# Slot rows of 272 floats instead of 257 in the two mixture stages of an eight-layer kernel

## The reference

```python
topk_idx, topk_w = _gate(xf, gate_w, gate_bias)        # 2 of 8 experts for each token
g = jax.nn.silu(jnp.einsum('th,ehi->tei', xf, w_gate)) # I = 128
u = jnp.einsum('th,ehi->tei', xf, w_up)
experts_y = jnp.einsum('tei,eih->teh', g * u, w_down)
masked_y = jnp.take_along_axis(experts_y, topk_idx[:, :, None], axis=1)
y = jnp.einsum('tkh,tk->th', masked_y, topk_w)
shared = jax.nn.silu(x @ sw_gate) * (x @ sw_up) @ sw_down
return y + shared
```

## Time and profile before

| | us |
|---|---|
| median of three runs | 3938.58 |
| the profiled execution | 3947.42 |
| its span, from the first to the last instruction | 3945.4 |
| PE busy | 3244.7 |
| DVE busy | 2616.1 |
| POOL busy | 1533.2 |
| mean granted TensorE clock | 0.917 of full speed |

### The profile page before, as it was taken

How to read it: one execution, slowest core, us unless ns; L and a number is a source line. 1 busy time by engine, 2 the same in 40 slices (tenths; PEclk the granted TensorE clock), 3 DMA queues, 4 the chain that set the end, 5 groups by cost and what they waited for, 6 DMA issues and landing times. The chain is left out here.

```text
span 3945.4 us, 55387 instructions
## 1 busy us (share of the span) xinstructions
PE 3244.7 (82%) x15992; PEld 1825.7 (46%) x15993; DVE 2616.1 (66%) x5017; ACT 1717.3 (44%) x3399; POOL 1533.2 (39%) x1586
## 2 busy tenths in 40 slices
PE   7898889888699698898979898776596787997495
PEld 3343334333256534434344466453374475664274
DVE  6999899999877585757668575974146673224145
ACT  5757666566355355554636553112032232222031
POOL 4898888988600212212121101534353100002533
PEclk8999999999999889798989999888798898998797
DMA  4555455565400000000000002601144792000236
GB/s 132 139 139 136 126 138 138 131 137 133 108 1 0 15 2 2 1 2 1 2 1 2 1 1 85 164 0 41 56 146 132 178 124 33 16 11 9 88 99 200
DMA packets 370273, 283.07 MB, mean 72 GB/s; under 512 B 214027, under 2 KB 290367, under 8 KB 370017
## 3 DMA queue, kind: packets, MB, share of 16 engines
q1 hardware_dynamic: 356960, 246.43, 25.5%
q0 software_dynamic: 13056, 33.65, 2.5%
HBM read 205.69 MB, written 76.16 MB: 71 GB/s over the span
## 5 line engine op out<-in xcount | busy, mean ns | idle before, releaser
L608 POOL TENSOR_TENSOR mamba_dBu<-mamba_du,mamba_bcs 128x512 f32<-128x512 f32 x512 | 640.3, 1272 | 127.6 <-DMA mamba_bcs<-mamba_bc 85.7
L531 PE MATMUL mamba_banks<-mamba_hc,ident 128*128 128x512 f32 x1024 | 537.8, 634 | 144.6 <-DVE mamba_hc L847 144.5
L777 ACT ACTIVATE mamba_banks<-mamba_delta,mamba_a_neg 128x512 f32<-128x512 f32 x512 | 352.3, 690 | 181.9 <-DVE mamba_hc L847 171.0
L1542 DVE TENSOR_REDUCE attn_mp<-attn_banks 128x1 f32<-128x512 f32 (+3 forms) x768 | 384.0, 551 | 69.0 <-PE attn_banks L1252 48.8
L531 PEld LDWEIGHTS mamba_banks<-mamba_hc,ident 128*128 128x128 f32 x1024 | 180.8, 195 | 459.1 <-DVE mamba_hc L847 346.6
L847 DVE TENSOR_TENSOR mamba_hc<-mamba_banks,mamba_bcs 128x512 f32<-128x512 f32 x512 | 344.3, 674 | 11.4 <-PE mamba_banks L531 11.4
L840 DVE TENSOR_TENSOR_SCAN mamba_banks<-mamba_banks,mamba_dBu 128x512 f32<-128x512 f32 x256 | 312.1, 1219 | 56.1 <-ACT mamba_banks L777 36.5
L840 DVE TENSOR_TENSOR_SCAN mamba_banks<-mamba_banks,mamba_h_end,mamba_dBu 128x512 f32<-128x512 f32 x256 | 327.3, 1279 | 20.1 <-ACT mamba_banks L777 12.2
L1249 PE MATMUL attn_banks<-attn_kT,attn_qT 96*128 96x512 bf16 (+3 forms) x768 | 272.3, 374 | 12.3 <-ACT attn_kT L1431 4.9
L1264 PE MATMUL attn_banks<-attn_qT,attn_kT 98*128 98x512 bf16 (+3 forms) x768 | 247.3, 341 | 12.5 <-ACT attn_r L1450 4.8
L939 PE MATMUL ffn_hp<-ffn_xT,ffn_w1T 128*128 128x512 f32 x512 | 231.3, 607 | 10.9 <-ACT ffn_xT L160 7.5
(11 more groups left out here) (389 smaller groups left out, 6665.9 us busy)
## 6 DMA issues: line engine op xcount, KB each, us to landing
mamba_bcs<-mamba_bc SPq DMA_DIRECT2D x256, 512.0 KB, 5.0
moe_slots_moe<-moe_pad SPq DMA_DIRECT2D x2, 9252.0 KB, 55.6
moe_xg<-moe_slots_moe SPq DMA_DIRECT2D x144, 128.5 KB
mix_qkv<-mixA_qkv SPq DMA_DIRECT2D x8, 1536.0 KB, 5.9
mixA_y<-moe_rows SPq DMA_DIRECT2D x16, 512.0 KB, 5.8
mix_qk<-mix_qkv SPq DMA_DIRECT2D x16, 512.0 KB, 7.7
mix_v<-mix_qkv SPq DMA_DIRECT2D x16, 256.0 KB, 7.6
mix_out<-mixB_oh SPq DMA_DIRECT2D x16, 256.0 KB, 6.9
```

The costliest lines, as they stand in the source:

```text
L531: pe.matmul(banks[:, SUMS + k % PAIR, :], c.ident[:, :], hc[:, n % RING, :], start=False, stop=True, skip_group_check=True).then_inc(sem(" ...
L608: pool.tensor_tensor(dBu[:, n % RING, :], du[:, v, k, :], bcs[:, i_of(n) % 4, 0, :], ALU.mult)\
L777: act.activation(banks[:, n % RING, :], delta[:, v, k, :], ACT.Exp, scale=a_neg[:, k, st:st + 1])\
L1542: dve.tensor_reduce(mp[:, qt // GT, j, qt % GT, at // 512:at // 512 + 1], banks[:, item % SLOTS, 0:size], AX.X, ALU.max).then_inc(sem("rin ...
```

## The change

`ROW` goes from `D + 1` = 257 floats (1028 bytes) to `D + 16` = 272 floats (1088 bytes, 17 times 64). The index stays at column `D`. What grows with it: the rows in DRAM of both `moe_slots` tensors, `moe_rows` (`xr`), `moe_xg`, and `moe_pad`. The 15 floats behind the index are zeroed once in each stage by a new memset on POOL, with a wait for it.

```diff
-ROW = D + 1
+LINE = 16
+ROW = D + LINE
@@
+        tail_ready = s.sem("tail_ready")
@@
                         pool.tensor_tensor(shift[:, at], minus[:, at], rstd[:, at], ALU.mult).then_inc(shift_ready, 1)
+                    pool.memset(xr[:, :, D + 1:ROW], 0.0).then_inc(tail_ready, 1)
+                    pool.wait_ge(tail_ready, 1)
                     pool.wait_ge(m["xd_padded"], 32)
@@
-                                pool.tensor_copy(xr[:, t:t + CHUNK, D:ROW].bitcast(U32).rearrange("p t o -> p (t o)"),
+                                pool.tensor_copy(xr[:, t:t + CHUNK, D:D + 1].bitcast(U32).rearrange("p t o -> p (t o)"),
@@
-                        pool.indirect_dma_start(yd, bass.IndirectOffsetOnAxis(ap=xg[:, i % XRING, D:ROW].bitcast(U32), axis=0),
+                        pool.indirect_dma_start(yd, bass.IndirectOffsetOnAxis(ap=xg[:, i % XRING, D:D + 1].bitcast(U32), axis=0),
@@
-    out["moe_pad"] = np.concatenate([np.zeros((P, D), np.float32), np.ones((P, 1), np.float32)], axis=1)
+    out["moe_pad"] = np.concatenate([np.zeros((P, D), np.float32), np.ones((P, LINE), np.float32)], axis=1)
```

## The result

The changed kernel took 3949.75 us (median of 20 runs), the kernel before took 3941.49 us on the same chip (median of 20). The ratio is 1.0017, with a 95% interval of 1.0009 to 1.0024: a small loss, 7 to 8 us, real but inside the 0.3% that the prediction counted as no change. The profiled execution of the changed kernel took 3957.95 us with a span of 3956.0 us.

A forecast was written before the change was run, and what follows sets the result against it. POOL's scatter issue, PE's shared expert, then the routed experts' ring were taken to bound the mixture stages. Slot loads -0.5, shifted tiles +1, the rest 0: +0.5 us, so 3939 us against the median, range 3923 to 3954.

The forecast's parts named there:

- Memset, scatters: Mixture stages on POOL: memset 0.41 us hidden in a 36 us wait, scatter issue unchanged at 0.960 us; both 0.
- The fill: Two DMAs in `lin` filling slot rows: 5.8% more bytes, landing long before POOL's only wait for it; 0 either way.
- The 77 and 58 us: The fill in `lin`: cost of 5.8% more bytes at 63.6 or 48.0 us a MB.
- The slot loads: Routed experts' ring: 22 waits, 15.5 us in all; each load 0.036 us less or 0.027 more; -0.5 us taken.
- the lower price: Slot loads: 48.0 us a MB, read from plain 1024-byte rows, against 55.2 for 1028-byte rows.
- the 15% for a packet: `mix_heads`: upper end for a dearer packet on shifted tiles, 1.26 us a set, 15 us over 12 sets.
- The tiles that move: `mix_heads` tiles shifted by 32 bytes: dearer packets would show as DVE store waits; 0 to +12 us, +1 taken.
- the 3 us that SP's queue was said to be able to fall behind: `mix_heads`: slack before DVE waits for a store, taken off the 15 us over 12 sets.
- The price of a packet: `mix_heads`: 12.4 ns a packet before; over 14 ns would show the prediction wrong.
- the case: Rival: `mix_heads` becomes bound by its DMAs, from about 15% a packet; 3961 us at 25%; chance 0.12 for over 0.3%.
- The rule of the Trainium skill: Pieces fetched from the 256-byte boundary below: slot loads +1.5 us in place of -0.5; `mix_heads` pieces some 20% more beats.
- The standstill: Rival: unaligned rows stop PE during the mixture stages' scatters; even rows save 83 us, 3856 us; chance 0.06.

The follow-up runs named there:

- rows-only kernel: The changed kernel with 224 bytes of unused SBUF ahead of the `mix` tiles, which so stand as before modulo 256 bytes; ratio 0.9995 to the kernel before.
- shift-only kernel: The kernel before, 257-float rows kept, with 32 bytes of unused SBUF ahead of the tiles of `mix`; ratio 1.0022.
- with four buffers: Four buffers of `mixB_oh` in place of two, a semaphore each; on one chip 3862.3 us on the changed kernel, 3861.3 us on the kernel before.
- `mixB_oh` alone: The kernel before with only `mixB_oh` shifted by 32 bytes, the other tiles in place modulo 256; ratio 1.0013.
- one-tile kernels: The kernel before with `mix_qk`, `mix_v` or `mixB_oh` alone shifted by 32 bytes; the three ratios add up to 1.0044.

## Why the prediction was right, and where a term was off

*Memset, scatters.* Right: 0.50 us (0.41 forecast) in a wait of 36 us; 0.960 us a scatter, as before.

*The fill.* Cost nothing, as said, and was dearer in neither of the two ways. Queue q1 over 80 us from the issue of the fill, changed kernel (2459:2539) and rows of 264 floats (2455:2535):

```profile
q1 hardware_dynamic: 19771, 20.59, 83.8%
```

```profile
q1 hardware_dynamic: 19723, 19.96, 80.0%
```

0.838 x 80 x 16 / 20.59 = 52.1 us a MB, and 51.3 for the 1056-byte rows, against 63.6 us; the 63.6 is the highest of the eight traces with 1028-byte rows, the others give 58.8 to 60.7 over the same 80 us. So a multiple of 32 bytes is enough. Longer rows landed sooner, and nobody waits for them. The 77 and 58 us in the prediction are sums that don't come out: 60 bytes on each of 18432 rows are 1.1 MB, 70 and 53 us at its two prices. Nothing hung on them.

*The slot loads.* -0.5 us was forecast, and the rows-only kernel is at 0.9995 (-2 us) in an interval of -6 to +2 us, so the sign isn't shown. The step behind it, that even rows take the lower price, failed. Queue q1 in the 24 us from the first slot load (2810:2834):

```profile
q1 hardware_dynamic: 1152, 1.11, 16.2%
```

0.162 x 24 x 16 / 1.11 = 56.0 us a MB, against 55.2 before, not the 48 of 1024-byte rows. Other traces with the same eight loads give 53.6 (rows-only) against 52.3 to 53.8 (257 floats), so the two kinds of row aren't told apart. The 48 was read where the queue's share was above 1, the 55.2 at a share of 0.15. So "rows that start at every multiple of 4 bytes cost 15% more a MB than even ones" fell with it, and with that the 15% for a packet had no base.

*The tiles that move.* The mechanism was right, with its place, its wait and its sign: a set every 8.87 us in place of 8.41, and DVE waiting for a store. The size was the mis-sized term: +1 us was taken of a range of 0 to +12, and the stretch grew by 8.4 us in the first pair of traces, the time by 1.0022 in the shift-only kernel, some 9 us. What failed is the sentence "the shift keeps every piece whole and at a multiple of 32, so I take +1 us, near the lower end". The start of long rows, from which I took it, says nothing of pieces of 64 and 128 bytes; for these a start at a multiple of 32 isn't enough, and at multiples of 64 nothing was lost. The upper end of 12 us held, but partly by luck: of its terms the 15% had no base, and no run shows the 3 us that SP's queue was said to be able to fall behind. SP's period rose by 5 to 7%. With these 5 to 7% the prediction's sum over 12 sets would be 2 to 4 us and not 8.4. In the traces SP's last load of `mix_qk` comes 6.0 us later in the stretch than before (3260.90 - 3145.9 against 3249.05 - 3140.0), so the slack of 3 us isn't there, and the other 2.4 us are lost behind that load; where, I haven't traced.

*The price of a packet* would have shown it, but far below the sign that the prediction named. It made 15% on a packet the point from which the case decides, and 14 ns the sign of it. Queue q1 over the whole head stretch and the median landing of `mix_qk`'s loads in it, before (3140:3293), after (3146:3308), then the changed kernel (3103:3255) and the kernel before (3100:3252) with four buffers:

```profile
q1 hardware_dynamic: 167296, 16.79, 88.9%
...
mix_qk<-mix_qkv SPq DMA_DIRECT2D x12, 512.0 KB, 7.2
```

```profile
q1 hardware_dynamic: 167296, 16.79, 85.8%
...
mix_qk<-mix_qkv SPq DMA_DIRECT2D x12, 512.0 KB, 7.9
```

```profile
q1 hardware_dynamic: 167296, 16.79, 91.5%
...
mix_qk<-mix_qkv SPq DMA_DIRECT2D x12, 512.0 KB, 8.0
```

```profile
q1 hardware_dynamic: 167296, 16.79, 88.8%
...
mix_qk<-mix_qkv SPq DMA_DIRECT2D x12, 512.0 KB, 7.0
```

0.889 x 153 x 16 / 167296 = 13.0 ns before and 0.858 x 162 x 16 / 167296 = 13.3 ns after; with four buffers 13.3 ns shifted and 12.9 in place. That is 2 to 3% on a packet. All five traces with a shifted `mix_qk` have 13.3 ns or more, loads of `mix_qk` that land after 7.7 to 8.1 us, and 8.7 to 9.0 us a set; eight of the nine others have 12.8 to 13.1 ns, 6.8 to 7.2 us and 8.3 to 8.5 us. The ninth, `mixB_oh` alone, fits neither: its cost (1.0013) goes with 12.5 ns a packet, loads that land after 7.3 us and 8.54 us a set, and its store's median landing is 7.5 us, the same as in the two other one-tile kernels. How its shift makes the store late stays open, and so does why a shifted piece is dearer to write.

*The rule of the Trainium skill* (DMA: Bandwidth & Descriptors, How a descriptor splits into AXI transactions) counts from the boundary of 256 bytes below a piece's start. The prediction worked it out for the first buffer of `mix_qk` only. Over all four buffers it gives `mix_qk`'s pieces a mean of 7 beats before and 8, 7 and 7 with 32, 64 and 128 bytes; `mixB_oh`'s 5, then 6, 5 and 5; `mix_v`'s 4, then 5, 6 and 4. For `mix_qk` and `mixB_oh` that agrees with the runs in what costs and what doesn't. For `mix_v` a shift by 64 bytes should be the dearest, and all three tiles together should stand at 18 beats against 16 before and 19 with 32 bytes; measured is 0.9999, with 12.9 ns a packet. Here the measurement decides, and it doesn't bear the rule out for the side where `mix_v`'s loads land. In size it is far off: 16 to 19 beats are 19%, measured were 2 to 3% on a packet. For the slot loads the rule gave +2.6% on the bytes fetched, so a dearer load (its +1.5 us counts all 128 loads, where the -0.5 us went by 22 waits); the traces above don't tell the sign.

*The standstill.* That even rows would end it (3856 us) was a rival at 0.06, and it is false: both kinds of row have it on one chip, neither on another, as the section above shows. Its working was sound, though: without the standstill the kernel takes 3863 us, 79 us less, where 83 us were worked out.

*The predicted 3939.0 us* stood on a median of three runs, 3938.58 us; the kernel before gave 3941.49 us in the 20 runs beside the changed one. Of the 10.75 us up to 3949.75, 2.9 us are this difference in the base, and the rest is the shift, less the 0.4 us forecast.

## What to carry to other kernels

When a kept buffer grows, look at where the allocator puts everything behind it: tiles that DMAs fill or read in pieces of 64 or 128 bytes should start on a multiple of 64 bytes, and 32 bytes of padding decide it. Before a shift is used to find a boundary, work out where the pieces of every buffer of the ring start; here 64 and 128 bytes changed nothing for two of the three tiles. Where a stage is as close to its bound as 8.4 to 8.0 us, more buffers for the tile whose store is waited for are worth a try. Four in place of two made this stage insensitive to the shift over its 16 sets, and showed whether the wait or the traffic was the bound: with the wait gone, the time that the issuing engine still needs for a set is its own. Before arguing from a long idle gap of an engine in one trace, look which engine took up ready work late, and whether another chip has the gap.

## What the runs showed of the hardware that I had not expected

- Small pieces and where they start in SBUF: a shift by 32 bytes costs 1.0022 (1.0011 to 1.0034), by 64 bytes 0.9999, by 128 bytes 1.0000. With four buffers for the store the same 32 bytes still slow SP from 8.41 to 8.99 us a set, though the kernels are only 1.0 us apart.
- PE stood still for 51.2 and 44.8 us during back-to-back indirect scatters in the first trace and not at all on two other chips, with the same code for this stage and the same pace of the scatters. ACT and DVE took up work there 12 to 53 us after it was ready. It is worth 2% of this kernel's time. What delays them is open.
- A fill with rows of 1056 or 1088 bytes costs 51.3 and 52.1 us of engine time a MB, with 1028 bytes 58.8 to 63.6 over eight traces.
